# Attention maxima run 26 score pairs ahead of the head, one in every group, and the first row of maxima turned in a spare bank

## The reference, cut to what matters

```python
xn = rms_norm(layernorm(x), gamma)
q, k, v = split(xn @ w_qkv)            # 16 heads of 64; w_qkv is 8 times its usual size
sim  = (q * 64 ** -0.5) @ k.T          # per head 2048 x 2048
attn = softmax(sim, axis=-1)           # so the maximum of every row of sim is subtracted
x    = x + (attn @ v) joined over heads @ w_out
```

## Time and profile before

| | |
|---|---|
| median of 3 runs | 2106.26 us (2103.5 to 2106.95) |
| the profiled execution | 2109.67 us, its span 2107.9 us |
| granted TensorE clock, mean of the span | 0.977 |
| PE busy | 1997.8 us (95%) |
| DVE busy | 1742.1 us (83%) |
| POOL busy | 1551.4 us (74%) |
| ACT busy | 1462.7 us (69%) |

### The profile page before, as it was taken

The page is one execution under the profiler, slowest core; times in us unless marked ns, Lnnn a source line. Parts: engine busy times, 40 slices in busy tenths (PEclk is TensorE's granted clock), DMA queues, the critical chain, the costliest instruction groups (busy, mean ns, idle before and its releaser), DMA issues.

```text
span 2107.9 us, 25599 instructions
## 1 busy us (share of the span) xinstructions
PE 1997.8 (95%) x8290; PEld 1411.5 (67%) x8290; DVE 1742.1 (83%) x1976; ACT 1462.7 (69%) x1804; POOL 1551.4 (74%) x771
## 2 busy tenths in 40 slices
PE   7999999997789999999999999999999999999987
PEld 5777776775566667666666766666676666666654
DVE  5777778655778998998899899889989988999855
ACT  4555455434277887887788788778878877888864
POOL 4333233232078999899899989989998998999992
PEclk9999999997799999999999999999999999999998
DMA  6201201310502130312213031221303122130000
GB/s 186 51 31 41 41 22 20 68 29 1 122 2 59 35 71 14 76 37 49 59 35 71 14 76 34 51 58 36 71 14 76 30 55 54 37 71 17 11 16 20
DMA packets 80679, 97.85 MB, mean 46 GB/s; under 512 B 33275, under 2 KB 36779, under 8 KB 80167
## 3 DMA queue, kind: packets, MB, share of 16 engines
q1 hardware_dynamic: 80550, 96.22, 20.5%
HBM read 44.25 MB, written 1.44 MB: 22 GB/s over the span
## 4 chain that ended last, share of the span: by engine, by line
PE 59%; DVE 6%; issue 3%; ACT 1%; POOL 1%; DVEq 0%; POOLq 0%
PE ps L889 10%; PE ps L911 10%; PE ps L912 10%; PE ps L926 9%; PE ps L929 9%; DVE m_part L1594 3%; PE ps L938 3%; PE ps L945 3%; DVE l_sum L1588 2%; ACT p_h L1267 1%; PE ps L871 1%; PE ps L872 1%; PE ps L873 1%; DVE xn L1566 0%; PE ps L897 0%
## 5 line engine op out<-in xcount | busy, mean ns | idle before, releaser
L635 POOL TENSOR_TENSOR p_l<-p_raw,p_h 128x1024 fp32r<-128x1024 f32 x512 | 1240.2, 2451 | 123.2 <-ACT p_h L1267 115.5
L1594 DVE TENSOR_REDUCE m_part<-ps 128x1 f32<-128x1024 f32 x512 | 622.1, 1217 | 142.5 <-PE ps L889 142.5
L1264 ACT ACTIVATE p_raw<-ps 128x1024 f32<-128x1024 f32 x512 | 567.1, 1108 | 208.7 <-PE ps L912 206.7
L1267 ACT ACTIVATE p_h<-ps 128x1024 fp32r<-128x1024 f32 x512 | 523.3, 1022 | 0.0
L911 PE MATMUL ps<-qa,ka 128*128 128x512 f32 x1024 | 441.2, 431 | 2.1 <-issue 1.4
L926 PE MATMUL ps<-p_h,v_hl 128*128 128x512 f32 x1024 | 403.2, 394 | 8.7 <-POOL p_l L635 7.1
L912 PE MATMUL ps<-qb,kb 65*128 65x512 f32 x1024 | 408.5, 399 | 0.0
L1588 DVE TENSOR_REDUCE l_sum<-p_raw 128x128 f32<-128x1280 f32 x256 | 377.2, 1476 | 11.0 <-ACT p_raw L1264 11.0
L889 PE MATMUL ps<-ka,qa 128*128 128x512 f32 x1024 | 339.1, 413 | 24.3 <-DVE m_part L1594 19.0
L929 PE MATMUL ps<-p_l,v_hl 128*64 128x512 f32 x1024 | 320.9, 394 | 0.0
L1576 DVE TENSOR_REDUCE p_raw<-p_raw 128x128 f32<-128x1024 f32 x256 | 308.9, 1210 | 9.1 <-ACT p_raw L1264 7.6
(11 more groups left out here) (200 smaller groups left out, 2303.1 us busy)
## 6 DMA issues: line engine op xcount, KB each, us to landing
g_bc<-g_scratch SPq DMA_DIRECT2D x64, 256.0 KB, 5.2
xn<-r_scratch SPq DMA_DIRECT2D x63, 256.0 KB, 4.2
qa<-qk_hi SPq DMA_DIRECT2D x112, 128.0 KB, 2.4
ka<-qk_hi SPq DMA_DIRECT2D x56, 128.0 KB, 2.4
kb<-qk_hi SPq DMA_DIRECT2D x56, 128.0 KB, 2.4
ka<-xn SPq DMA_DIRECT2D x28, 128.0 KB, 2.3
qb<-xn SPq DMA_DIRECT2D x28, 128.0 KB, 2.3
ka<-qk_low SPq DMA_DIRECT2D x28, 128.0 KB, 2.8
```

The source lines that it names most:

```text
L635: nc.gpsimd.tensor_tensor(p_l[:, g % 4, :, :], slots(g), p_h[:, g % 4, :, :].bitcast(fp32), ALU.subtract).then_inc(pl_done, 1)
L1264: af(slots(g), s_t, ACT.Exp).then_inc(raw_done, 1)
L1267: af(p_h[:, g % 4, :, :], s_t, ACT.Exp).then_inc(ph_done, 1)
L1594: nc.vector.tensor_reduce(m_part[:, it, half:half + 1], ps[:, first_bank:first_bank + 2, :].rearrange("p b n -> p (b n)"), AX.X, ALU.max). ...
```

## The change

The 22 pairs ahead become 26, and every group of a window has one pair: the last six of the head in 0.0 to 0.5, those of the next head from 0.6 on. The sixteenth pair of the next head now lies in 2.5, so `maxima_end` for part 0 moves from 3.2 to 2.6 and the turn from 3.3 to 2.6, where it uses chunk 2's spare bank. The fourth `v` projection makes room: it goes from 2.6 to 2.4. `maxima_end` for part 1 moves from 1.2 to 0.6; its turn stays in 1.5. SP moves the first row at the end of its list for chunk 2 and no longer in chunk 3. The opening computes 26 pairs, the last window 6.

```diff
-REST_OF_MAXIMA = ((1,) * 8, (1, 1, 0, 0, 0, 0, 0, 0), (0,) * 8, (0,) * 8)
-NEXT_MAXIMA = ((0,) * 8, (0, 0, 1, 1, 1, 1, 1, 1), (1,) * 8, (1, 1, 1, 0, 1, 1, 1, 2))
+REST_OF_MAXIMA = ((1, 1, 1, 1, 1, 1, 0, 0), (0,) * 8, (0,) * 8, (0,) * 8)
+NEXT_MAXIMA = ((0, 0, 0, 0, 0, 0, 1, 1), (1,) * 8, (1,) * 8, (1,) * 8)
 AHEAD = sum(map(sum, NEXT_MAXIMA))
...
-         ((3, "v", 2), (5, "sums", 0), (6, "v", 3), (7, "out", 0)),
+         ((3, "v", 2), (4, "v", 3), (5, "sums", 0), (6, "turn", 0), (7, "out", 0)),
...
-REST_END, NEXT_END, NEXT_TURN = (1, 2), (3, 2), (3, 3)
-TURN_BANK, OPENING_TURN = 4, 18
-TURN_AT = AHEAD - sum(NEXT_MAXIMA[NEXT_TURN[0]][NEXT_TURN[1]:])
+REST_END, NEXT_END = (0, 6), (2, 6)
+OPENING_TURN = 18
...
+                if kind == "turn" and n == 0 and not has_next:
+                    continue
...                                        # SP, window()
-                    if c == NC - 1 and not last:
-                        maxima_row(head + 1, 1 - par, 0)
                     if exists(summed[0]):
                         store_sums(*summed)
                         load_sums(*summed)
                     if c == 1:
                         maxima_row(head, par, 1)
+                    elif c == 2 and not last:
+                        maxima_row(head + 1, 1 - par, 0)
...                                        # PE, evicted()
-                    pe.wait_ge(mt_done, 2 * head + 2)
+                    pe.wait_ge(mt_done, 2 * (head + 1 - n) + n + 1)
...                                        # PE, main_chunk()
-                    if (c, g) == (NEXT_TURN[0], NEXT_TURN[1] + 1) and has_next:
-                        pe.wait_ge(mt_done, 2 * head + 3)
...
-                    if (c, g) == NEXT_TURN and has_next:
-                        pe.wait_ge(s_max, PRIME + MAXIMA * (head + 1) + TURN_AT)
-                        turn_maxima(head + 1, 1 - par, 0, TURN_BANK)
...
-                            turn_maxima(head, par, 1, spare)
+                            turn_maxima(head + 1 - n, par if n == 1 else 1 - par, n, spare)
...                                        # ACT, main_chunk(), likewise
-                            turn_maxima(head, 1, spare_bank(c))
+                            turn_maxima(head + 1 - n, n, spare_bank(c))
...
-                    if (c, g) == NEXT_TURN and has_next:
-                        turn_maxima(head + 1, 0, TURN_BANK)
```

## The result

The changed kernel takes 2090.03 us (median of 4 runs, 2088.71 to 2092.74). The kernel before took 2106.61 beside it (4 runs). The ratio is 0.9924, 95% interval 0.9907 to 0.9941, so it is 12.4 to 19.6 us faster. The forecast was 2084.0. The profiled executions took 2109.67 and 2092.74, their spans 2107.9 and 2090.9, so 17.0 less against a forecast of 22.2.

A forecast was written before the change was run, and what follows sets the result against it. PE bounds the middle chunks, POOL just behind, and DVE's queue the boundaries between windows. Boundaries -26.6, opening +5.1 and last window -0.7 sum to -22.2 us, taking the profiled 2109.67 to 2087.5 and the median to 2084.0; range 2077 to 2095.

The forecast's parts named there:

- C: Chunk 2: turn finds maxima or bank late, or two v projections wait on each other; 6 us, 2090; chance 0.08.
- D: Opening: four more pairs may keep the low clock into the first window, +6, 2090, or the opposite, -2; chance 0.06.
- The boundary: Between windows: without 3.7's second pair DVE reaches 0.0's maximum 2.06 us sooner, so both PE waits go.
- 3.3 and 3.4: Chunk 3: pair added +0.46, turn gone -0.52, wait for ACT's copy gone -0.25; sum -0.31 us.
- The turn in chunk 2: Group 2.6: the turn moved there costs +0.52 us of PE, its possible waits costed at 0.
- Odd windows: Boundaries into odd windows 1 to 13, priced like window 14: -1.85 us each.
- Even windows: Boundaries into windows 2 to 12: -1.65 us each, 0.2 subtracted for PE's wait for POOL in 1.3.
- The opening: Ahead of the first window: four more pairs cost +4.6 to +5.1 us, +5.1 taken, from maxima 1.27 apart.
- The last window: Four groups (0.6 to 1.1) lose a pair, 1.86 us of PE, most lost to POOL's pace; -0.7 taken.
- A: POOL takes over: its low parts delay the values, boundary gain lost, opening paid; +4.4, 2110.7; chance 0.05.
- B: DVE stays late at boundaries: ACT's copy or a pair comes 0.6 late, each boundary keeps 1.25; 2093; chance 0.12.
- E: More than forecast: waits left in 0.2 to 0.4 go too, even windows keep all; -28, 2078; chance 0.09.

The follow-up runs named there:

- e1_double: Changed kernel with chunk 3's old pairs back (none in 3.3, two in 3.7), turn kept in 2.6; 2109.32 us, ratio to before 1.0006.
- e2_turn: Changed kernel, one pair in every group, but the first row turned in bank 4 in 3.3 and moved in chunk 3, as before; 2105.57 us, ratio 0.9994.
- e7_ahead: Changed kernel keeping only the 26 pairs ahead; chunk 3's pairs and the turn in 3.3 as before the change; 2112.26 us, ratio 1.0023.
- e6_filler: Changed kernel with two unused matmuls behind each opening pair from the eleventh on; 2088.19 us, ratio 0.9906.
- e3_opening: Changed kernel with 22 opening pairs; window 0 catches up with two pairs each in 1.3, 1.4, 2.3 and 2.4; 2087.83 us, ratio 0.9908.
- e4_wv: Changed kernel with POOL making the low part of the v weights in group 1.0, not 1.1; 2073.73 us, ratio 0.9836.
- e5_both: Changed kernel with 22 opening pairs, two pairs each in window 0's groups 0.0 to 0.3, and the edit of e4_wv; 2076.15 us, ratio 0.9852.
- e8_best: e4_wv with the opening's filler of e6_filler; 2070.31 us, ratio 0.9832.
- e9_before_wv: Kernel before the change with the low part of the v weights behind group 1.0; 2095.65 us, ratio 0.9952.

## Why the prediction was right, and what it missed

The time lies in the range (2077 to 2095), the sign and the mechanism are as forecast, and the gain is smaller by a quarter. In the spans: forecast -22.2, measured -17.0. The forecast's own narrower range, 2079 to 2088, was missed by 2. Rivals C and D had 2090, which is the time measured, but not by what they describe, as the terms show.

**The boundary** (-2.06). Right. 3.7 lost 1.13, 0.1 lost 0.87, both waits are gone, DVE's queue is 3.28 long, and e1_double brings them back. Together 2.00.

**3.3 and 3.4** (-0.31). Too much by 0.15: from 6.69 to 6.54. The wait in 3.4 was sized right (3.62 to 3.38, 0.24 for 0.25); the miss is in 3.3, which with a pair for the turn takes 3.16, where 3.02 is the plain cost.

**The turn in chunk 2** (+0.52). Right: 0.53, with no wait, so rival C is out.

**Odd windows** (-1.85). The seven lost 12.13, 1.73 each; 0.8 us in all missing. Window 14 lost 1.47, 0.4 missing.

**Even windows** (-1.65). The five of 2 to 10 lost 8.30, 1.66 each. Window 12 lost 0.07. PE's timeline there, kernel after, and the stretches around:

```profile
1708.97 0.39 PE L927 MATMUL ps<-p_h,v_hl 128*128 128x512 f32 x1
1710.51 0.30 PE L872 MATMUL ps<-wv_hl,x_h 128*128 128x128 f32 x1 [1.15 <-POOL wv_hl L652]
```

```profile
1706.80:1712.20 5.40, 4.25 (x25) 3.16 (x24) 4.52 (x4) 3.30 (x5) 5.40 (x5) 1.00 0.00 0
1712.20:1717.20 5.00, 5.00 (x14) 2.65 (x13) 2.35 (x2) 2.72 (x4) 5.00 (x4) 0.66 0.00 0
```

The granted clock falls behind the wait and the short matmuls of `v`, to 0.66 on the mean of five microseconds of full work, and 1.4 takes 4.97 and not 3.42. The same wait without the fall stands in the other windows, so this is 1.6 us that differ from one window, and one profile, to the next. No step of the sum has it.

**The opening** (+5.1). 4.45 in the profile. The term was sized by maxima 1.27 apart at the low clock, but from 579.2 to 585.9 the kernel after had 1.00, and its last pairs start 1.13 apart, which gives 4.5 for four. The seven profiled kernels with 26 pairs have 35.3 to 37.0, the four with 22 have 30.7 to 31.9.

**The last window** (-0.7 beside its share of a boundary). Right: it lost 1.60, and the sum implied 0.9 of the boundary and 0.7.

**Window 0**: this is the term that failed. The sum gave it the end of a boundary and the turn, some -0.9; it was +0.80. The step that was off is the one that took window 0 as undisturbed and put its clock into rival D at 0.06. D said that "four more such pairs may keep the lower level into the first window". The level was low there, at 0.50 for ten microseconds, but not kept: the last seven microseconds of the opening had 1.00, and the fall came where the window starts. D's price was too high as well. Its groups of 4.3 us have ten matmuls each, but the first three of window 0 have six, since the values come three groups later, and the first four lost 1.37 in all, not 6. Group 0.7 gave 1.38 back, because in the kernel before PE waited there for ACT's exponentials (1.56 us). What remained came later, 0.3 in 1.3 and 1.3 in 1.4, where a fall that the kernel before has too (0.81 from 618 to 624) lasted longer. That is no single case: 1.3 and 1.4 take 12.5 together in the kernel after, e1_double, e2_turn and e7_ahead, all with 26 pairs and a low clock at the window's start, 10.9 in the kernel before and 9.4 in e6_filler. Why that fall lasts longer is open.

The Trainium skill (TensorE: Matmul & The Clock Gate, Part 1) has the clock slow by default and released by activity. From this the prediction had taken that the low stretch would last to the window's own matmuls. The trace of the kernel after differs: the clock came back in the opening, at 1.00 from 579.2 to 585.9 with PE busy for 3.67 of 6.70 us, and then stood at 0.50 with PE busy for 9.72 of 10.

**The tail**, from the last scores to the end, was 1.36 longer (67.71 for 66.35). It lies between 64.1 and 67.8 over all profiles, without order, and no step of the prediction treats it. What lies ahead of the opening differs as much, 544.1 to 552.9 us, but is alike in these two (549.8 and 549.9).

Together: window 0 1.7, window 12 1.6, tail 1.36, odd windows and 14 1.2, less 0.65 in the opening: 5.2, the gap between -22.2 and -17.0. Window 12 and the tail, 3.0 of it, are of the kind that another profile of the same kernel may not show. Of the rivals, A is out (POOL has 2.56 of idle time left in the odd window, and PE is busy for all but 0.04 of it), B is out (no wait before L1560), and E is out (1.8 at most for a boundary). Left open is what decides whether the clock falls after the wait in 1.3 of a given window: the kernel after, e2_turn, e6_filler and e7_ahead had such falls past window 0, the kernel before, e1_double and e3_opening had none, each in one profile. Of the 42 such windows, 2 to 12 of these seven kernels, six had one, each in group 1.4. Left open too is what lets the clock fall at the start of window 0.

## What to carry to other kernels

When one edit makes room for another, cost and test them together: here either alone gave 0.2 or 0.4 us for a window and both gave 1.66, because the pair could leave 3.7 without a new wait only once the turn had left 3.3. A wait that other engines set, as POOL's here, keeps its length when everything else gets shorter; look for the instruction ahead of it that could change places, which was worth as much as the change. And price the start of a loop by itself: work moved ahead of it is paid there in full (about 4.4 us for these four pairs, on the mean of all profiles), and the first window behind it is not like the others: here it lost nothing where they lost 1.7.

## What the runs showed of the hardware that was not expected

- The granted clock fell in full work behind a short wait. PE had waited 1.15 us and then ran twelve matmuls of 128 columns; it then had 0.66 for five microseconds. No kernel with the wait removed (e4_wv, e5_both, e8_best, e9_before_wv) showed such a fall past window 0, in 24 windows where the seven others had six in 42.
- Under like work the clock of the opening and of the window's start differed between profiles. In the kernel after, pairs that waited 0.40 each for DVE left PE busy for 6.55 of 10 us, at a mean clock of 0.84, and the window behind them ran at 0.50 for ten microseconds, though PE was busy for 9.72 of them. In e4_wv the same pairs, with PE busy for 6.18 of 10 us, ran at 1.00, and the next ten microseconds had 0.83.
- Two filling matmuls for each pair cost the opening nothing: 35.82 and 35.30 from the first pair to the window, where the five kernels with 26 pairs and no filler have 35.3 to 37.0. Whether they do anything for the clock is not shown.
- Taking away a wait of 1.2 us on the mean in seven places (8.6 in all) gave 16.3 us in the medians; by the profiles about half of it lies in window 0 and in a fall of the clock that went with the wait.
